# A cross-attention and soft-MoE kernel on one core: new order of loads, layer norm, query products and ctx turns in its opening

## The chip, the cores and the metric

The kernel runs on one core of one Trainium2 chip. The metric is the device time of one execution in microseconds (us); lower is better. The median of three runs of the kernel before is 443.7 us (443.57 to 444.12).

## What is computed

All arrays are float32: `x` is 8 x 56 x 128, `ctx_1024` is 8 x 1500 x 128, Wq, Wk and Wv are 128 x 1024 (16 heads of 64), Wo is 1024 x 128.

```
q = heads(_layernorm(x) @ Wq);  k = heads(ctx @ Wk);  v = heads(ctx @ Wv)
attn = softmax(q @ k.T * 64 ** -0.5)                     # 8 batches, 16 heads, 56 x 1500
x = x + (attn @ v) @ Wo
logits = (_layernorm(x) @ phi_w.T + phi_b).reshape(8, 56, 64, 32)
D, C = softmax(logits, axis=3), softmax(logits, axis=2)
X_tilde = clip(einsum('tznp,tzd->npd', D, x), -33000, 65000)    # of the normalised x
X_tilde = tanh(layernorm over d of X_tilde)
Y_tilde = einsum('npd,ndH->npH', X_tilde, expert_w) + expert_b
x = x + einsum('tznp,npH->tzH', C, Y_tilde)
```

## The kernel before

The five engines have an instruction list each (`@block.sync`, `gpsimd`, `tensor`, `scalar`, `vector`), written out by hand, and semaphores alone order them against each other. An engine takes its list strictly in order, so an instruction that waits holds up everything behind it.

**Attention.** The weights are folded first: `wqk` holds, per head, Wq times Wk transposed (128 x 128), and `wvo` the product of Wv and Wo. So a score is (normalised x) @ wqk @ ctx transposed, and the big per-batch operand is ctx itself. For a batch `b` the 16 x 56 = 896 query rows are cut into NT = 7 tiles of 128 rows (`t`, and `g = 7 b + t`), and the 1500 keys into KB = 3 banks of 500, a bank being 4 chunks (CPB) of 125 keys. Each float32 operand is split into a rounded high part and the rest: ScalarE writes the high part (`hi_ctx`, `hi_qk`, `hi_probs`), VectorE the low part (`lo_ctx`, `lo_qk`, `lo_probs`), and TensorE multiplies hi x hi, hi x lo, lo x hi. A tile is: nine score matmuls into the three `scores` banks (`make_scores`), a row maximum per bank on VectorE (`row_max`), one exponential over 1500 columns on ScalarE (`exp_tile`), twelve transposes of the probabilities (`turn_probs`), and a share of the product with ctx (`context_product`). The scores of tile g+1 wait for the exponential of tile g, since they write the same banks.

**The opening**, which the change rewrites, makes what tile 0 needs. SP's queue issues x, three 125-row thirds of the first ctx (`ctx_raw`, one per bank, 250 KB each), Wv and Wo; ScalarE's queue issues Wq and Wk. VectorE makes the layer norm of x in four columns of two batches each (`layernorm(0, x_sb, 0, NQ)`, NQ = 4; the power -0.5 is on GpSimd, `root`), giving `xn`. TensorE, in order: turns Wq (banks S0, S1) and Wk (S2, T0), turns ctx bank 0, turns the four blocks of `xn` into bank ACC (`xnT`), turns ctx bank 1, makes the head products of the first eight heads (`head_pairs(wqT, wkT, 0, T1, S0)`), turns ctx bank 2, and makes the first quarter of the queries (`make_qk(0, 0)`, four heads for the first pair of batches). Each result is copied out of its bank by ScalarE (counted by `setup_act`) or VectorE (`setup_dve`). `setup_pe` counts TensorE's own steps. Quarter `r` of the queries is needed from the tile that first touches its heads: quarter 0 for tile 0, quarter 1 for tiles 1 and 2, quarter 2 for tile 3, quarter 3 for tile 5.

**The rest of the setup** is spread over the first tiles of batch 0 (`half(0, first=True)`), behind the transposes of the tile before: in tile 0 `make_qk(1)`, the other eight heads' `head_pairs`, half of Wv turned, `make_qk(2)`; in tile 1 the other half of Wv, `make_qk(3)`; in tiles 2 and 3 the four `head_products` for `wvo` and two turns of batch 1's ctx; in tile 4 the third turn. GpSimd makes the untransposed split of ctx (`split_ctx`), which also frees `ctx_raw` for the next load, and from `split_qk(1)` on the queries of later batches.

The lines that matter most, on TensorE before tile 0:

```
turn_ctx(0, 0, 1, first=True)
pe.wait_ge(xn_ready, 1)
for q in range(NQ):
    last = tr(bank(ACC)[:, PT * q:PT * q + PT], xn[:, q, :], ident[0:PT, 0:PT])
last.then_inc(setup_pe, 1)
turn_ctx(0, 1, 0, first=True)
pe.wait_ge(setup_act, 3)
head_pairs(wqT, wkT, 0, T1, S0)
```

Lines in the profile: L355 to L360 are SP's first loads, L1043 and L1044 ScalarE's; L612 `turn_weight`, L591 `turn_ctx`, L646 the turn of `xn`, L628 and L632 `head_pairs`, L597 `make_qk`, L667 to L669 `make_scores`, L679 `turn_probs`, L1057 `hi_ctx`, L1063 and L1064 `hi_qk`, L1050 and L1051 ScalarE's copies, L1083 the exponential, L1275 to L1288 the layer norm, L1299 and L1300 VectorE's copies, L1306 `lo_ctx`, L1313 `lo_qk`, L1320 and L1323 `row_max`.

Of the kernel before, what the change touches and what calls it, by code (L numbers as in the profile page):

```python
# [12 lines left out]
def xattn_softmoe_kernel(  # L13
# [63 lines left out]
    with ExitStack() as ctx:  # L77
# [329 lines left out]
        def _(pool):  # L407
# [117 lines left out]
            root(0, 0, NQ)  # L525
# [54 lines left out]
        def _(pe):  # L580
# [61 lines left out]
            turn_weight(wk_sb, 1, T0)  # L642
            turn_ctx(0, 0, 1, first=True)
            pe.wait_ge(xn_ready, 1)
            for q in range(NQ):
                last = tr(bank(ACC)[:, PT * q:PT * q + PT], xn[:, q, :], ident[0:PT, 0:PT])  # L646
            last.then_inc(setup_pe, 1)
# [1 line left out]
            pe.wait_ge(setup_act, 3)
            head_pairs(wqT, wkT, 0, T1, S0)  # L650
            pe.wait_ge(ctxT_lo, 1)
            turn_ctx(0, 2, 1, first=True)
# [962 lines left out]
```

## Time and profile before

| | us |
|---|---|
| median of three runs (lowest, highest) | 443.7 (443.57, 444.12) |
| the profiled execution, its own time | 445.9 |
| its span in the trace | 444.1 |
| TensorE busy in the span | 426.5 |
| VectorE, ScalarE, GpSimd busy | 332.0, 245.2, 159.8 |

The profiled execution took 445.9 us, 2.2 above the median; 1.8 of its time lie outside the span. All positions below are microseconds from the start of the span. A row of a timeline gives start, duration, engine, line, operation, output and input; a row with `xN` stands for N like instructions, its duration from the first's start to the last's end. In brackets stand the idle time before and what ended it. PE is TensorE's matmul, PEld its weight load, DVE VectorE, ACT ScalarE, POOL GpSimd; SPq and ACTq are the queues of those engines, on which a load is issued.

### The profile page before, as it was taken

Reading aid. Unit: us, or ns where it says so; the run is one execution under the profiler, and the core shown is the slowest. Engines: PE = TensorE matmul, PEld = TensorE weight load, DVE = VectorE, ACT = ScalarE, POOL = GpSimd, SP = SyncE. Lnnn points to the kernel's source line nnn. Section 1 sums busy time; section 2 is a strip of 40 time slices with the busy share of each in tenths; the row PEclk is TensorE's granted clock in tenths of the full one; section 3 lists DMA queues with packets and bytes.
Section 4 is the critical chain, followed back from the end, with each engine's and each line's share of the span. In section 5 each row is a group of like instructions: output and inputs, shape, how many; then the busy total and the mean of one; then the engine's idle time right before and its main releaser. Section 6 shows DMA issues by size and latency. Waiting matters only on the chain.

```text
span 444.1 us, 7406 instructions
## 1 busy us (share of the span) xinstructions
PE 426.5 (96%) x2990; PEld 390.2 (88%) x2990; DVE 332.0 (75%) x606; ACT 245.2 (55%) x413; POOL 159.8 (36%) x88
## 2 busy tenths in 40 slices
PE   3899999999999999999999999999999999899997
PEld 2788899999999999889999998899999888798986
DVE  2567775776687678857898789978988999659871
ACT  2266556566565556655665566556656565533641
POOL 2509800416040213130716134517140342456740
PEclk9999999999999999999999999999999999899999
DMA  8111020014111001110010011000000000296000
GB/s 218 63 70 13 13 78 12 13 71 112 13 13 71 19 12 13 70 19 12 11 74 18 13 11 73 19 13 14 1 19 13 11 2 18 56 243 177 1 1 22
DMA packets 15110, 19.05 MB, mean 43 GB/s; under 512 B 3954, under 2 KB 10882, under 8 KB 15076
## 3 DMA queue, kind: packets, MB, share of 16 engines
q1 hardware_dynamic: 14788, 17.53, 15.1%
q10 hardware_dynamic: 288, 1.05, 0.8%
q8 instruction: 24, 0.39, 0.4%
q14 instruction: 10, 0.08, 0.1%
HBM read 18.32 MB, written 0.26 MB: 42 GB/s over the span
## 4 chain that ended last, share of the span: by engine, by line
PE 78%; DVE 10%; ACT 5%; issue 2%; DMA 2%; POOL 2%; POOLq 1%; ACTq 0%
PE turned L679 15%; PE scores L667 8%; PE acc L699 8%; PE acc L701 8%; PE acc L700 8%; PE scores L669 8%; PE scores L668 8%; PE misc L716 3%; DVE small L1320 2%; PE misc L741 2%; DVE pT_l L1330 2%; PE misc L591 2%; ACT prob L1083 2%; DMA wk_sb<-in_L_xattn_Wk_dram 2%; ACT pT_h L1076 1%
## 5 line engine op out<-in xcount | busy, mean ns | idle before, releaser
L1076 ACT CAST pT_h<-turned 125x512 fp32r<-125x512 f32 x168 | 95.0, 590 | 123.8 <-PE turned L679 123.3
L1330 DVE TENSOR_TENSOR pT_l<-turned,pT_h 125x512 fp32r<-125x512 f32 x168 | 112.3, 687 | 65.6 <-ACT pT_h L1076 64.6
L1320 DVE TENSOR_REDUCE small<-scores 128x1 f32<-128x500 f32 x168 | 108.6, 674 | 7.0 <-PE scores L669 6.6
L679 PE MATMUL turned<-ident,prob 128*125 128x128 f32 x672 | 94.5, 276 | 2.9 <-DVE pT_l L1330 2.6
L679 PEld LDWEIGHTS turned<-ident,prob 128*125 128x125 f32 x672 | 87.5, 187 | 10.3 <-DVE pT_l L1330 4.3
L699 PE MATMUL acc<-pT_h,ctx_nh 125*128 125x256 f32 (+1 forms) x288 | 94.9, 330 | 0.0
L1083 ACT ACTIVATE prob<-scores,small 128x1500 f32<-128x1500 f32 x56 | 84.9, 1516 | 13.0 <-DVE small L1323 12.6
L701 PE MATMUL acc<-pT_h,ctx_nl 125*128 125x256 f32 (+1 forms) x288 | 87.1, 303 | 0.0
L700 PE MATMUL acc<-pT_l,ctx_nh 125*128 125x256 f32 (+1 forms) x288 | 87.0, 302 | 0.0
L667 PE MATMUL scores<-ctx_th,qk_h 128*128 128x500 f32 x168 | 67.8, 403 | 1.9 <-DVE qk_l L1313 1.2
L669 PE MATMUL scores<-ctx_th,qk_l 128*128 128x500 f32 x168 | 65.3, 389 | 0.0
L668 PE MATMUL scores<-ctx_tl,qk_h 128*128 128x500 f32 x168 | 65.0, 387 | 0.0
L699 PEld LDWEIGHTS acc<-pT_h,ctx_nh 125*128 125x128 f32 x288 | 55.3, 192 | 0.0
L700 PEld LDWEIGHTS acc<-pT_l,ctx_nh 125*128 125x128 f32 x288 | 55.2, 192 | 0.0
L701 PEld LDWEIGHTS acc<-pT_h,ctx_nl 125*128 125x128 f32 x288 | 55.0, 191 | 0.0
L427 POOL TENSOR_TENSOR ctx_nh<-ctx_raw,zero 125x1536 fp32r<-125x1536 f32 x8 | 22.0, 2749 | 89.3 <-PE acc L701 83.4
L667 PEld LDWEIGHTS scores<-ctx_th,qk_h 128*128 128x128 f32 x168 | 31.6, 188 | 7.6 <-issue 3.0
L669 PEld LDWEIGHTS scores<-ctx_th,qk_l 128*128 128x128 f32 x168 | 31.5, 188 | 6.4
L668 PEld LDWEIGHTS scores<-ctx_tl,qk_h 128*128 128x128 f32 x168 | 31.7, 189 | 4.4
L501 POOL TENSOR_TENSOR logit<-logit,cmax 112x2048 f32<-112x2048 f32 (+1 forms) x5 | 18.5, 3699 | 34.1 <-DVE cmax L1386 32.5
L431 POOL TENSOR_TENSOR ctx_nl<-ctx_raw,ctx_nh 125x1536 fp32r<-125x1536 f32 x8 | 28.0, 3494 | 0.6
L493 POOL TENSOR_TENSOR logit<-logit,cmax 112x2048 f32<-112x2048 f32 (+1 forms) x4 | 16.5, 4130 | 16.8 <-DVE cmax L1410 16.3
(179 smaller groups left out, 544.1 us busy)
## 6 DMA issues: line engine op xcount, KB each, us to landing
ctx_raw<-in_ctx_dram SPq DMA_DIRECT2D x7, 750.0 KB
rbc<-rden_row SPq DMA_DIRECT2D x15, 128.0 KB, 3.0
rbc<-rden_row SPq DMA_DIRECT2D x8, 192.0 KB, 3.0
eb<-in_L_ffn_expert_b_dram SPq DMA_DIRECT2D x4, 256.0 KB, 5.6
ctx_raw<-in_ctx_dram SPq DMA_DIRECT2D x3, 250.0 KB
wq_sb<-in_L_xattn_Wq_dram ACTq DMA_DIRECT2D x1, 512.0 KB, 5.0
wk_sb<-in_L_xattn_Wk_dram ACTq DMA_DIRECT2D x1, 512.0 KB, 8.3
wv_sb<-in_L_xattn_Wv_dram SPq DMA_DIRECT2D x1, 512.0 KB, 9.1
```

What stands on the lines that cost most here:

```text
L431: gp.tensor_tensor(ctx_nl[a][:, :, :], ctx_raw[:, :, :], ctx_nh[a][:, :, :].bitcast(F32), ALU.subtract).then_inc(ctx_nat, 1)
L667: mm(o, hi, ctx_th[a][:, keys], start=True, stop=False)
L668: mm(o, hi, ctx_tl[a][:, keys], start=False, stop=False)
L669: mm(o, lo, ctx_th[a][:, keys], start=False, stop=True).then_inc(scores_pe, 1)
L679: last = tr(turned[0:CK, m, 128 * c:128 * c + 128], prob[u][:, CK * j:CK * j + CK], ident[:, :])
L699: mm(o, ctx_nh[a][:, j, :], hi, start=(j == 0), stop=False)
L700: mm(o, ctx_nh[a][:, j, :], lo, start=False, stop=False)
L701: last = mm(o, ctx_nl[a][:, j, :], hi, start=False, stop=(j == NC - 1))
L1076: nc.scalar.copy(pT_h[0:CK, PLACES[g // NT % 2][t], CPB * k:CPB * k + CPB, :], turned[0:CK, (KB * u + k) % 2, :].rearrange("p (c r) -> p c ...
L1083: nc.scalar.activation(prob[u][:, :].rearrange("p (k w) -> p k w", k=KB), scores[:, :, 0:KW], ACT.Exp, bias=negmax[:, u:u + 1], accum_out= ...
L1320: m = v.tensor_reduce(bankmax[:, u, k:k + 1], scores[:, k, 0:KW], AX.X, ALU.max)
L1330: v.tensor_tensor(pT_l[0:CK, place, dst, :], turned[0:CK, (KB * u + k) % 2, :].rearrange("p (c r) -> p c r", c=CPB), pT_h[0:CK, place, dst ...
```

## The change

Loads: SP now issues x and Wk. ScalarE issues Wq, then each third of the first ctx as two loads, of rows 0 to 111 and 112 to 124, then Wv and Wo. Layer norm: the first column (the first pair of batches) is made and applied by itself, the other three behind it. TensorE before tile 0: Wq, Wk, one block of `xn`, ctx bank 0, head products, ctx bank 1, query quarter 0 (into bank ACC), and then, behind the wait for the split queries, ctx bank 2; the scores of each bank of tile 0 wait for that bank's ctx alone. The other three blocks of `xn` are turned at the end of tile 0. Wv's turns and query quarters 2 and 3 move to tiles 1 and 2, and the turns of batch 1's ctx to tiles 3 and 4 (two of them in tile 4). ScalarE makes the exponential of tile 0 before its copy of the second half of `wqk`.

```diff
             sp.dma_start(x_sb[:, :, :], x_v).then_inc(x_in, 16)
-            for k in range(KB):
-                chunks = slice(CPB * k, CPB * k + CPB)
-                sp.dma_start(ctx_raw[:, chunks, :], ctx_v[0][:, chunks, :]).then_inc(ctx0_in[k], 16)
-            sp.dma_start(wv_sb[:, :], Wv).then_inc(wvo_in, 16)
-            sp.dma_start(wo_sb[:, :, :], Wo.rearrange("(j p) n -> p j n", p=128)).then_inc(wvo_in, 16)
+            sp.dma_start(wk_sb[:, :], Wk).then_inc(wk_in, 16)
...
             act.dma_start(wq_sb[:, :], Wq).then_inc(wq_in, 16)
-            act.dma_start(wk_sb[:, :], Wk).then_inc(wk_in, 16)
+            for k in range(KB):
+                chunks = slice(CPB * k, CPB * k + CPB)
+                for p0, p1 in ROW_PARTS:
+                    act.dma_start(ctx_raw[p0:p1, chunks, :], ctx_v[0][p0:p1, chunks, :]).then_inc(ctx0_in[k], 16)
+            act.dma_start(wv_sb[:, :], Wv).then_inc(wvo_in, 16)
+            act.dma_start(wo_sb[:, :, :], Wo.rearrange("(j p) n -> p j n", p=128)).then_inc(wvo_in, 16)
...
-            root(0, 0, NQ)
+            root(0, 0, 1)
+            root(1, 1, NQ)
             split_ctx(0, 0, first=True)
...
+                    if g == 0:
+                        pe.wait_ge(ctxT_lo, k + 1)
+                        if k == 0:
+                            turn_ctx(0, 2, 1, first=True)
...
                         if t == 0:
-                            make_qk(1, 1)
-                            pe.wait_ge(setup_dve, 1)
+                            make_qk(1, M0)
                             head_pairs(wqT, wkT, 2, T0, T1)
+                            pe.wait_ge(qk_lo, 1)
+                            pe.wait_ge(xn_ready, 2)
+                            turn_xn(1, NQ)
+                        if t == 1:
+                            pe.wait_ge(xnT_dve, 2)
                             pe.wait_ge(wvo_in, 32)
                             turn_weight(wv_sb, 0, ACC)
-                            pe.wait_ge(setup_act, 5)
-                            pe.wait_ge(setup_dve, 4)
-                            pe.wait_ge(qk_lo, 1)
-                            make_qk(2, 0)
-                        if t == 1:
-                            pe.wait_ge(setup_act, 6)
-                            turn_weight(wv_sb, 1, ACC)
                             pe.wait_ge(qk_lo, 2)
-                            make_qk(3, 1)
+                            turn_weight(wv_sb, 1, M0)
+                            make_qk(2, M1)
...
                         if t == 4:
-                            pe.wait_ge(setup_dve, 7)
-                            turn_ctx(1, 2, 1)
+                            pe.wait_ge(setup_dve, 6)
+                            turn_ctx(1, 1, 1)
+                            pe.wait_ge(ctxT_lo, KB + 1)
+                            turn_ctx(1, 2, 0)
...
             hi_ctx(0, 0, 0, 1)
+            copy_out(5, wqk[:, 0:8:2, :], T1, SCALE)
             hi_ctx(0, 0, 1, 0)
-            copy_out(6, wqk[:, 0:8:2, :], T1, SCALE)
+            hi_qk(0, ACC)
             hi_ctx(0, 0, 2, 1)
-            hi_qk(0, 0)
-            hi_qk(1, 1)
-            copy_out(8, wqk[:, 8:16:2, :], T0, SCALE)
+            hi_qk(1, M0)
...
-            layernorm(0, x_sb, 0, NQ)
-            layernorm_apply(0, x_sb, xn, 0, NQ, xn_ready)
+            layernorm(0, x_sb, 0, 1)
+            layernorm(1, x_sb, 1, NQ)
+            layernorm_apply(0, x_sb, xn, 0, 1, xn_ready)
```

How the order of the instructions moves, from Wk's turns to tile 0 on TensorE. Before:

```order
L612 MATMUL turned<-ident,wk_sb 128x128 x4
L591 MATMUL misc<-ident,ctx_raw 128x125 [waits ctx0_in0]
L591 MATMUL misc<-ident,ctx_raw 128x125 x3
L646 MATMUL acc<-ident,xn 128x112 [waits xn_ready]
L646 MATMUL acc<-ident,xn 128x112 x3
L591 MATMUL misc<-ident,ctx_raw 128x125 [waits ctx0_in1]
L591 MATMUL misc<-ident,ctx_raw 128x125 x3
L628 MATMUL turned<-wkT,wqT 128x128 [waits setup_act]
...
L591 MATMUL misc<-ident,ctx_raw 128x125 [waits ctx0_in2,ctxT_lo]
L591 MATMUL misc<-ident,ctx_raw 128x125 x3
L597 MATMUL misc<-xnT,wqk 128x112 [waits ctxT_lo,setup_dve,setup_act]
L597 MATMUL misc<-xnT,wqk 128x112 x3
L667 MATMUL scores<-ctx_th_61,qk_h_63 128x500 [waits qk_lo,ctxT_lo]
```

The same stretch of TensorE with the change:

```order
L613 MATMUL turned<-ident,wk_sb 128x128 x4
L640 MATMUL acc<-ident,xn 128x112 [waits xn_ready]
L592 MATMUL misc<-ident,ctx_raw 128x125 [waits ctx0_in0]
L592 MATMUL misc<-ident,ctx_raw 128x125 x3
L629 MATMUL turned<-wkT,wqT 128x128 [waits setup_dve,setup_act]
...
L592 MATMUL misc<-ident,ctx_raw 128x125 [waits ctx0_in1]
L592 MATMUL misc<-ident,ctx_raw 128x125 x3
L598 MATMUL acc<-xnT,wqk 128x112 [waits xnT_dve,setup_dve,setup_act]
L598 MATMUL acc<-xnT,wqk 128x112 x3
L592 MATMUL misc<-ident,ctx_raw 128x125 [waits ctx0_in2,ctxT_lo,qk_lo]
L592 MATMUL misc<-ident,ctx_raw 128x125 x3
L675 MATMUL scores<-ctx_th_61,qk_h_63 128x500
```

Three turns of `xn` and one of ctx's banks no longer stand ahead of the head products (L628, now L629), and the third ctx turn stands behind the first query product and behind the wait for `qk_lo`.

ScalarE, from its start to the first exponential. Before:

```order
L1043 DMA wq_sb<-in_L_xattn_Wq_dram 128x1024
L1044 DMA wk_sb<-in_L_xattn_Wk_dram 128x1024
L1051 ACT_TABLE_LOAD
L1051 COPY wqT<-scores 128x512 [waits setup_pe] x2
...
L1063 COPY qk_raw<-misc 128x224 [waits qk_pe]
L1064 CAST qk_h_63<-misc 128x224
L1050 ACTIVATE wqk<-turned 128x4x128 [waits setup_pe]
L1083 ACTIVATE prob_51,small<-scores,small 128x1500 [waits negmax_dve]
```

With the change:

```order
L1053 DMA wq_sb<-in_L_xattn_Wq_dram 128x1024
L1057 DMA ctx_raw<-in_ctx_dram 112x512
L1057 DMA ctx_raw<-in_ctx_dram 13x512
...
L1058 DMA wv_sb<-in_L_xattn_Wv_dram 128x1024
L1059 DMA wo_sb<-in_L_xattn_Wo_dram 128x8x128
L1066 ACT_TABLE_LOAD
...
L1078 COPY qk_raw<-misc 128x224 [waits qk_pe]
L1079 CAST qk_h_63<-misc 128x224
L1098 ACTIVATE prob_51,small<-scores,small 128x1500 [waits negmax_dve]
L1065 ACTIVATE wqk<-turned 128x4x128 [waits setup_pe]
```

Nine loads instead of two stand ahead of the table load, and the copy of `wqk` stands behind the exponential.

## Rows read from the trace of the kernel before

**Rows 1.** The page's first part: busy time, share of the span and instructions of each engine.
```profile
PE 426.5 (96%) x2990; PEld 390.2 (88%) x2990; DVE 332.0 (75%) x606; ACT 245.2 (55%) x413; POOL 159.8 (36%) x88
```

**Rows 2.** Busy time by stretch, cut at the tiles' first scores; the last three: PEclk, DMA share, GB/s.
```profile
core 0: us, PE busy (x) PEld busy (x) DVE busy (x) ACT busy (x) POOL busy (x), PEclk, DMA share, GB/s
0.00:5.80 5.80, 0.00 (x0) 0.02 (x1) 0.00 (x0) 1.28 (x1) 1.21 (x10) 1.00 0.63 187
5.80:9.50 3.70, 1.94 (x8) 1.55 (x8) 1.96 (x12) 1.17 (x2) 1.03 (x1) 1.00 1.03 279
...
18.83:25.33 6.50, 5.94 (x45) 5.02 (x46) 3.27 (x6) 2.83 (x6) 2.33 (x1) 1.00 0.16 56
...
30.31:36.58 6.27, 6.14 (x41) 5.39 (x42) 4.77 (x10) 3.64 (x8) 3.57 (x2) 1.00 0.01 0
...
43.14:49.96 6.82, 6.65 (x43) 5.73 (x44) 5.08 (x9) 4.12 (x8) 6.74 (x5) 1.00 0.01 4
...
70.00:380.00 310.00, 309.04 (x2045) 283.63 (x2044) 249.67 (x439) 181.55 (x299) 100.80 (x37) 1.00 0.11 27
```

**Rows 3.** The chain that ended last, from 0 to 40 us: start, duration, what.
```profile
1.16 8.32 DMA wk_sb<-in_L_xattn_Wk_dram
...
9.52 1.12 PE scores L612 x4
...
11.49 0.83 PE misc L591 x4
12.32 0.75 PE acc L646 x4
...
13.90 0.51 PE turned L628
...
16.52 1.13 PE misc L597 x8
...
18.83 0.47 PE scores L667
```

**Rows 4.** The timeline from 0 to 30 us: the loads' issues, the table load and GpSimd's first split.
```profile
1.15 1.14 SPq L358 DMA_DIRECT2D ctx_raw<-in_ctx_dram  x3
...
1.69 1.28 ACT L1051 ACT_TABLE_LOAD   x1 [1.69 <-PEq L1602]
...
3.06 1.54 SPq L360 DMA_DIRECT2D wo_sb<-in_L_xattn_Wo_dram  x1
...
14.86 2.75 POOL L427 TENSOR_TENSOR ctx_nh<-ctx_raw,zero 125x1536 fp32r<-125x1536 f32 x1 [5.92 <-DMA ctx_raw<-in_ctx_dram]
```

**Rows 5.** The same timeline: turns, copies and splits on TensorE, ScalarE and VectorE.
```profile
5.81 1.94 PE L612 MATMUL scores<-ident,wq_sb 128*128 128x128 f32 x8 [5.81 <-DMA wq_sb<-in_L_xattn_Wq_dram]
...
8.97 1.12 DVE L1288 TENSOR_SCALAR xn<-x_sb,lnmv,lnrs 112x128 f32<-112x128 f32 x4 [1.14 <-POOL lnrs L470]
...
15.57 0.65 PE L591 MATMUL misc<-ident,ctx_raw 125*128 125x125 f32 x4
15.68 0.60 ACT L1050 ACTIVATE wqk<-turned 128x512 f32<-128x512 f32 x1 [1.16 <-PE scores L632]
...
16.87 0.68 DVE L1306 TENSOR_TENSOR ctx_tl<-misc,ctx_th 128x500 fp32r<-128x500 f32 x1 [0.46 <-ACT ctx_th L1057]
17.67 0.35 ACT L1063 COPY qk_raw<-misc 128x224 f32<-128x224 f32 x1 [0.83 <-PE misc L597]
...
18.30 0.39 DVE L1313 TENSOR_TENSOR qk_l<-misc,qk_h 128x224 fp32r<-128x224 f32 x1 [0.75 <-ACT qk_h L1064]
...
21.85 0.16 DVE L1323 TENSOR_REDUCE small<-small 128x1 f32<-128x3 f32 x1
...
23.59 1.50 ACT L1083 ACTIVATE prob<-scores,small 128x1500 f32<-128x1500 f32 x1
```

**Rows 6.** The table by stretch again, while batch 1's ctx is loading alone.
```profile
24.00:26.00 2.00, 1.72 (x11) 1.50 (x12) 0.00 (x0) 2.00 (x5) 0.00 (x0) 1.00 0.32 130
```

**Rows 7.** The timeline from 30 us: the end of GpSimd's split of the weights.
```profile
46.06 0.67 POOL L464 TENSOR_TENSOR xa_l<-xnT,xa_h 128x224 fp32r<-128x224 f32 x1
```

More of the change, by code:

```diff
@@ L592, in turn_ctx, with make_qk @@
                 last.then_inc(ctxT_pe, 1)
-            def make_qk(r, m):
+            def make_qk(r, k):
                 for c in range(4):
-                    last = mm(misc[:, m, PT * c:PT * c + PT], wqk[:, 4 * r + c, :],
+                    last = mm(bank(k)[:, PT * c:PT * c + PT], wqk[:, 4 * r + c, :],
                               xnT[:, 0:PT], start=True, stop=True)
@@ L634, in head_pairs, with turn_xn @@
                 second.then_inc(setup_pe, 1)
+            def turn_xn(q0, q1):
+                for q in range(q0, q1):
+                    last = tr(bank(ACC)[:, PT * q:PT * q + PT], xn[:, q, :], ident[0:PT, 0:PT])
+                last.then_inc(xnT_pe, 1)
             pe.wait_ge(ident_ready, 1)
@@ L642, in _ @@
             turn_weight(wk_sb, 1, T0)
+            pe.wait_ge(xn_ready, 1)
+            turn_xn(0, 1)
             turn_ctx(0, 0, 1, first=True)
[L644 to L647, printed above, removed]
+            pe.wait_ge(setup_act, 3)
+            pe.wait_ge(setup_dve, 1)
+            head_pairs(wqT, wkT, 0, T1, S0)
             turn_ctx(0, 1, 0, first=True)
[L649 to L652, printed above, removed]
             pe.wait_ge(setup_act, 4)
-            pe.wait_ge(setup_dve, 3)
-            pe.wait_ge(ctxT_lo, 2)
-            make_qk(0, 0)
+            pe.wait_ge(setup_dve, 2)
+            pe.wait_ge(xnT_dve, 1)
+            make_qk(0, ACC)
             def make_scores(g, a, t):
@@ L1057, in hi_ctx, with hi_qk @@
                 nc.scalar.copy(ctx_th[a][:, KW * k:KW * k + KW], misc[:, m, 0:KW]).then_inc(ctxT_hi, 1)
-            def hi_qk(r, m):
+            def hi_qk(r, k):
                 act.wait_ge(qk_pe, r + 1)
-                both = misc[:, m, 0:4 * PT].rearrange("p (h b t) -> p b h t", h=4, b=2)
+                both = bank(k)[:, 0:4 * PT].rearrange("p (h b t) -> p b h t", h=4, b=2)
                 nc.scalar.copy(qk_raw[:, 4 * r:4 * r + 4, :], both[:, 1])
@@ L1307, in lo_ctx, with lo_qk @@
                                 ALU.subtract).then_inc(ctxT_lo, 1)
-            def lo_qk(r, m):
+            def lo_qk(r, k):
                 dve.wait_ge(qk_hi, r + 1)
-                both = misc[:, m, 0:4 * PT].rearrange("p (h b t) -> p b h t", h=4, b=2)
+                both = bank(k)[:, 0:4 * PT].rearrange("p (h b t) -> p b h t", h=4, b=2)
                 hs = slice(4 * r, 4 * r + 4)
@@ L1494, in half, with copy_xnT @@
                         if t == 0:
[L1495 to L1497 removed]
+                            lo_qk(1, M0)
+                            copy_out(8, wqk[:, 9:16:2, :], T1, SCALE)
+                            copy_xnT(1, NQ)
                         if t == 1:
[L1499 to L1500 removed]
+                            copy_out(10, wvT[:, 4:8, :], M0)
+                            lo_qk(2, M1)
                         if t == 2:
[L1502 to L1503 removed]
+                            lo_qk(3, M0)
+                            copy_out(12, wvo[:, 8:16:2, :], M1)
                         if t == 3:
[L1505 to L1506 removed]
+                            lo_ctx(1, 1, 0, 0)
+                            copy_out(14, wvo[:, 9:16:2, :], M1)
                         if t == 4:
[L1508 removed]
+                            lo_ctx(1, 1, 1, 1)
+                            lo_ctx(1, 1, 2, 0)
+            def copy_xnT(q0, q1):
+                dve.wait_ge(xnT_pe, 2 if q0 else 1)
+                v.tensor_copy(xnT[:, PT * q0:PT * q1], bank(ACC)[:, PT * q0:PT * q1]).then_inc(xnT_dve, 1)
             copy_out(4, wkT[:, 4:8, :], T0)
+            copy_xnT(0, 1)
+            layernorm_apply(1, x_sb, xn, 1, NQ, xn_ready)
+            copy_out(6, wqk[:, 1:8:2, :], S0, SCALE)
             lo_ctx(0, 0, 0, 1)
[L1512 to L1513 removed]
             lo_ctx(0, 0, 1, 0)
[L1515 removed]
+            lo_qk(0, ACC)
             lo_ctx(0, 0, 2, 1)
[L1517 removed]
             for b in range(B):
```

80 lines of the change are left out of this document (36 added, 44 removed).

## The prediction

> **What bounds the kernel.** I read the page's busy times first: TensorE is busy 426.5 of 444.1 us, the next engine 332.0 [rows 1]. The table by stretch says where the rest is: between 70 and 380 us TensorE idles for 1.0 of 310 us, while in the first 9.5 us it has 1.94 us of work, and in the tile from 18.83 to 25.33 it idles for 0.56 [rows 2]. So the body is bound by TensorE, and the change removes no work of TensorE's. It can only start that work earlier, close gaps in the opening, and do less of it at the slow clock. What it wins there is kept to the end as long as nothing else becomes late, since the body has no slack to swallow it.
>
> The chain of waits gives the opening's order: Wk's load from 1.16 to 9.5, then TensorE without a break (Wk's turns from 9.52, ctx, `xn`, ctx, head products from 13.83), then the copy of `wqk`, the first queries at 16.52, their split, and the scores at 18.83 [rows 3]. Wq's turns had begun at 5.81 and, at 0.22 us each, were all issued by 7.5 [rows 5]. TensorE then stood for 2.0 us for Wk.
>
> The granted clock reads 1.00 throughout [rows 2], but four turns take 1.12 us at 9.52 and 0.65 us at 15.57 [rows 3, 5]. By these durations the engine ran at 1.2 GHz first and was at 2.4 GHz by 15.57.
>
> I compare starts of the tiles. Before, the scores begin at 18.83 (tile 0), 25.33, 30.31, 36.58, 43.14 and 49.96 (tile 5) [rows 2]; the text names the gain at each.
>
> **1. Wk earlier.** By 5.8 us the loads have moved 5.8 x 187 = 1.08 MB and by 9.5 another 3.7 x 279 = 1.03 MB, 2.12 MB in all [rows 2]. ScalarE's queue held only Wq and Wk, 1.05 MB, and the second landed at 9.5: the two queues moved equal amounts. Now SP's queue holds x and Wk, 0.75 MB. If the queues share alike again, Wk has landed when 1.51 MB are through, at 5.8 + 0.43 / 0.279 = 7.3 us. If ctx gets the larger share and is all in before Wk, 2.05 MB are, at 9.3 us. I take 8.0, near the first, because it is what the rows show of the sharing, with something added for ctx's smaller pieces. Wk's turns start at 8.05: gain 1.5 (bounds 2.0, as TensorE is free at 7.5, and 0.2).
>
> The split of ctx into 112 and 13 rows: while a 125-row load runs alone, the DMA share is 0.32 and 130 GB/s move [rows 6], against 1.03 and 279 with many loads [rows 2]: a third of the engines. With all of them on it, ctx's 0.75 MB are in by 9.3 (the far end of step 1), against 14.86, when GpSimd got the last third [rows 4]. TensorE needs the thirds at about 9.9, 12.6 and 15.6, so it doesn't wait for them. The Trainium skill ("DMA: Bandwidth & Descriptors", how many engines) has a load run on the largest number up to 16 that divides its rows, 5 for 125, 16 for 112, 13 for 13: 5 of 16 is 0.31, and the rows agree. The same page's rules for kernel authors speak against two transfers to disjoint halves of the partitions ("Don't bother"), as both use the same engines; by that rule the first third comes no sooner than before, and the result is the third rival's.
>
> **2. Less ahead of the head products.** From Wk's first turn to the head products stood 4.31 us of turns: eight of Wk, four of ctx, four of `xn`, four of ctx [rows 3]. Three of `xn` (three quarters of 0.75) and the second ctx group (0.83) move behind: 4.31 - 0.56 - 0.83 = 2.9, with ends 2.7. The head products start at 10.8 against 13.83. They now also wait for VectorE's copy of Wk's second half, about 0.7 us after the turns at 9.75, hidden by the ctx turns (until 10.75). The layer norm is not late: all four columns were ready at 8.97 + 1.12 = 10.1 [rows 5], the first of them 0.8 before that, and TensorE wants the first at 9.75. Gain 3.0.
>
> **3. To the first scores.** Before, 5.0 us from 13.83 to 18.83. The second ctx group goes into the gap in which TensorE waits for the copy of `wqk` (0.60 us, [rows 5]), where the third stood before: nothing. The third comes behind the split queries and ahead of the first scores: 0.45 us at the full clock (0.65 with the last one's tail, [rows 5]), on the path. Scores at 10.8 + 5.0 + 0.45, less some 0.15 that TensorE no longer waits for `lo_ctx`: 16.1. Gain 2.7.
>
> **4. The third bank.** Its ctx must pass ScalarE (0.58) and VectorE (0.68) after 16.25, so its scores run 17.6 to 18.3, and VectorE's maximum is ready at 19.7 against 22.0 [rows 5]. The split costs 1.1 us between first scores and maximum less what VectorE waited: gain 2.3.
>
> **5. The first exponential.** Before, it began at 23.59, 1.6 after its maximum, behind ScalarE's copy of `wqk` [rows 5]. That copy is now behind it, and `hi_qk(1)` ahead: quarter 1 is multiplied from 18.3, in 1.1 us [rows 3], and its two copies take 0.6 (17.67 to 18.30, [rows 5]). So the exponential starts at 20.0, and tile 1 at 21.75 against 25.33: gain 3.6. TensorE has half a Wv turn (0.45) and a query quarter (0.9) less to do in tile 0 and three turns of `xn` more, and idles some 0.9 us.
>
> **6. Giving back.** What was left out comes later. Tile 1 has one more Wv turn: 5.4 against 4.98 us, gain at tile 2 3.15. Tile 2 has 6.2 us of matmuls and a ScalarE copy of 0.6 ahead of its query copies: 6.35 against 6.27. Tiles 3 and 4 as before: gain at tile 5 2.9 to 3.0. Tile 4 has two ctx groups in place of one: 0.45 on TensorE, but 0.6 on ScalarE and 0.7 on VectorE, each ahead of tile 5's maximum. Tile 5 keeps 2.5 to 2.9.
>
> **What isn't on the path.** GpSimd gets its first split 5 us earlier. Quarter 3's split comes 2 us later, and so `split_qk(1)` and `split_weights`, which were done at 46.7 [rows 7]; batch 1 needs them only seven tiles of some 6 us behind 16.1, at 58. ScalarE issues nine loads, not two, ahead of its table load. At 0.38 us each for six ctx loads (three took 1.14), 0.7 for Wv and 1.54 for Wo [rows 4] it is done at 5.7 and has its table (1.28) by 7.0, when the first turned bank waits: nothing or 0.3, with 2 us of slack at the head products.
>
> **Sum.** 2.7 us of gain at tile 6, carried to the end: the profiled execution would go from 445.9 to 443.2, the median from 443.7 to **441.0**. Bounds: Wk at 7.5 adds 0.5. The clock may rise before the head products, which halves 1.7 us of them and what follows at the slow clock: up to 0.9. That gives 4.1 and 439.6. Wk at 9.3 takes 1.3 and the pile-up in tile 4 up to 0.6: 0.8 and 442.9. Range 439.4 to 443.0.
>
> **Rivals.**
> - *Wk is late again* (ctx on ScalarE's queue takes most of the engines' time). For it: ctx's rows are short pieces and all of them stand in the queue beside Wk. Against it: the equal shares so far. Wk at 9.3, gain 1.4: 442.3. Chance 0.12.
> - *More than the sum*: Wk by 7.5, so that TensorE runs without a gap from 5.8 on and reaches 2.4 GHz some microseconds earlier. For it: before, it had 2 us of standing in that stretch. Gain 3.9: 439.8. Chance 0.18.
> - *The split buys nothing*: a piece of 112 rows goes on few engines like one of 125. The first third is turned at 11.3 as before [rows 3], not at 9.9. Against it: x's and Wk's rows, 112 and 128, ran at the full share of 1.03 [rows 2]. Gain 1.3: 442.4. Chance 0.05.
> - *Given back*: tile 4's second ctx group and the later GpSimd chain cost what was won. For it: VectorE and ScalarE set the pace there more than TensorE (6.65 busy of 6.82, [rows 2]). Against: 2.7 us are a lot for 0.7 us of work. 443.3. Chance 0.05.
> - *Slower: ScalarE is held by its loads.* Wo's issue took 1.54 us, not 0.3 [rows 4], perhaps because the queue was full. If eight of the nine took that, ScalarE is free at 13.5, has its table at 14.8, its three copies by 16.6, and the head products start at 16.7. The path behind them is as in steps 3 to 6: 3.2 us slower, 446.9. It decides from the point at which the head products start later than 13.5, so from ScalarE free at 10.4. Against it: in SP's queue the three ctx issues together took 1.14. Chance 0.05.
>
> **Chances.** Forecast 0.55, the rest as above. A measurement of this kernel can tell about 0.2%, 0.9 us, from no change. Faster takes the forecast and the first three rivals: 0.90. Same 0.05, slower 0.05.
>
> **What the new profile should show.** Wk's turns start at 7.6 to 8.5 (at 9.3, the first rival); head products at 10.8; the first scores at 16.1; the exponential at 20.0; tile 1 at 21.7, tile 5 at 47.1; the body as busy as before. ctx's thirds all in before 10, seen on GpSimd's first split. The table load starts at about 5.7; if it starts after 10, the slower rival holds. I am wrong in substance if tile 1 is early and tile 6 isn't.

## The result and the profile after: 1.2% slower

The changed kernel takes 449.94 us (median of 4 runs, 448.61 to 450.21). The kernel before, beside it, takes 443.81 (443.57 to 444.12). The ratio is 1.0116, 95% interval 1.0087 to 1.0145. The forecast was 441.0, in a range of 439.4 to 443.0: the sign was wrong. The profiled execution of the new kernel took 448.61 with a span of 446.8.

The page's first part of the new kernel, beside [rows 1]:

```profile
PE 427.2 (96%) x2990; PEld 390.4 (87%) x2990; DVE 336.7 (75%) x608; ACT 245.2 (55%) x413; POOL 160.2 (36%) x89
```

TensorE has the same work. VectorE has two instructions more and is busy for 4.7 us more: some instruction of VectorE's has become long. The table by stretch, of the new kernel, shows where TensorE lost its time (after the busy times: PEclk, DMA share, GB/s):

```profile
0.00:9.00 9.00, 2.33 (x10) 1.97 (x11) 1.95 (x11) 2.45 (x3) 2.66 (x12) 1.00 0.78 229
9.00:11.00 2.00, 2.00 (x12) 2.00 (x11) 0.39 (x1) 0.59 (x1) 0.60 (x1) 1.00 1.00 310
11.00:14.00 3.00, 3.00 (x21) 2.45 (x20) 3.00 (x4) 0.94 (x2) 2.92 (x2) 1.00 0.54 137
14.00:17.70 3.70, 0.63 (x5) 0.28 (x3) 3.70 (x4) 0.81 (x2) 2.66 (x1) 1.00 0.00 0
17.70:25.00 7.30, 6.19 (x21) 5.19 (x22) 3.46 (x6) 1.17 (x3) 0.00 (x0) 0.53 0.12 36
...
21.14:28.35 7.21, 6.47 (x38) 5.29 (x37) 4.34 (x8) 2.81 (x6) 0.00 (x0) 0.73 0.26 96
28.35:33.46 5.11, 5.11 (x37) 4.76 (x38) 2.88 (x5) 2.70 (x5) 0.00 (x0) 1.00 0.06 21
33.46:40.24 6.78, 6.78 (x49) 5.97 (x47) 5.03 (x11) 4.44 (x9) 0.00 (x0) 1.00 0.01 0
...
46.84:53.66 6.82, 6.82 (x47) 6.10 (x48) 5.08 (x9) 4.11 (x8) 6.82 (x4) 1.00 0.01 4
53.66:60.21 6.55, 5.98 (x39) 5.26 (x40) 5.05 (x10) 4.10 (x8) 6.47 (x5) 1.00 0.00 0
...
70.00:380.00 310.00, 309.06 (x2046) 283.69 (x2045) 248.38 (x440) 183.22 (x302) 98.41 (x36) 1.00 0.11 28
```

From 14.0 to 17.7 TensorE works for 0.63 us, while VectorE is busy without a break. In the 7.3 us after that the granted clock is 0.53. The first scores (tile 0) start at 21.14, where the kernel before had 18.83 [rows 2], and tile 1 starts at 28.35 against 25.33. The body from 70 to 380 us is as busy as before. By tile 55, the last one (374.63 against 370.39), the kernel is 4.24 us behind.

The chain that ended last names the hole (start, duration, what):

```profile
1.15 7.41 DMA wk_sb<-in_L_xattn_Wk_dram
...
8.60 1.12 PE scores L613 x4
...
11.59 0.51 PE turned L629
...
13.60 1.02 PE misc L592 x4
14.63 3.07 issue
17.69 1.60 PE acc L598 x8
...
21.49 0.42 PE scores L675
```

Wk's turns at 8.60 and the head products at 11.52 to 11.59 are early, against 9.52 and 13.83 to 13.90 [rows 3]. At 14.63 the product for the first queries (`make_qk`, L598) stands for 3.07 us. "issue" gives no releaser. The timeline does:

```profile
7.73 0.34 DVE L1303 TENSOR_SCALAR xn<-x_sb,lnmv,lnrs 112x128 f32<-112x128 f32 x1
...
10.40 2.75 POOL L426 TENSOR_TENSOR ctx_nh<-ctx_raw,zero 125x1536 fp32r<-125x1536 f32 x1 [1.62 <-DMA ctx_raw<-in_ctx_dram]
...
10.61 0.69 DVE L1316 COPY wkT<-turned 128x512 f32<-128x512 f32 x1 [2.54 <-PE turned L613]
11.22 0.26 DVE L1530 COPY xnT<-acc 128x112 f32<-128x112 f32 x1
11.40 5.59 DVE L1303 TENSOR_SCALAR xn<-x_sb,lnmv,lnrs 112x128 f32<-112x128 f32 x3
...
13.23 3.43 POOL L430 TENSOR_TENSOR ctx_nl<-ctx_raw,ctx_nh 125x1536 fp32r<-125x1536 f32 x1
...
16.91 0.68 DVE L1315 TENSOR_SCALAR wqk<-scores 128x512 f32<-128x512 f32 x1
```

The query product needs VectorE's half of the `wqk` copy (L1315). That copy stands behind the three `xn` instructions of the layer norm (L1303), and these take 5.59 us, where four took 1.12 before [rows 5]. The summary of this tile has their durations in ns, as lowest, median and highest:

```profile
L1303 DVE TENSOR_SCALAR xn<-x_sb,lnmv,lnrs x3: 333/1832/3583, 11.4 to 16.7; 112x128 f32<-112x128 f32 x3
```

The 1.83 us from 11.4 on end at about 13.2, where GpSimd's first split instruction (L426) ends; the 3.58 end as its second (L430) does, at 16.66. Behind L430 GpSimd is idle, and the last `xn` takes its usual 0.33. VectorE is shown as busy and not as waiting, so no list of waits points to GpSimd.

Each `xn` instruction reads and writes SBUF, as GpSimd's do. The two copies from PSUM, at 10.61 and 11.22, ran at their usual length beside the same GpSimd instruction. That gave my theory.

**Theory.** The change makes two pieces collide that had never met. The new loads bring ctx in by 10.24 instead of 14.69, which starts GpSimd's split at 10.40 instead of 14.86 [rows 4]. The new order on VectorE puts three quarters of the layer norm behind the copy of Wk, at 11.40. VectorE is then held until each GpSimd instruction ends, TensorE stands for 3.1 us, and the clock falls after that.

**Rivals.** The new loads themselves are at fault; the new order on the engines is; or the split of ctx into 112 and 13 rows is.

### The profile page after: what moved, and what is told of

It reads as the page before. It is cut to its first block, busy times and chain, and to the rows that moved or that the text cites. A ratio compares the mean times of both kernels' runs of the same rounds, so it can differ in the third digit from the quotient of the medians.

```text
span 446.8 us, 7415 instructions
## 1 busy us (share of the span) xinstructions
PE 427.2 (96%) x2990; PEld 390.4 (87%) x2990; DVE 336.7 (75%) x608; ACT 245.2 (55%) x413; POOL 160.2 (36%) x89
## 3 DMA queue, kind: packets, MB, share of 16 engines
q1 hardware_dynamic: 13358, 16.24, 14.2%
## 4 chain that ended last, share of the span: by engine, by line
PE 78%; DVE 10%; ACT 5%; issue 3%; POOL 2%; DMA 2%; POOLq 1%; SPq 0%
PE turned L687 15%; PE scores L675 8%; PE scores L677 8%; PE scores L676 8%; PE acc L707 8%; PE acc L709 8%; PE acc L708 8%; PE misc L724 3%; PE misc L592 2%; DVE small L1336 2%; PE misc L749 2%; DVE pT_l L1346 2%; ACT prob L1098 2%; DMA wk_sb<-in_L_xattn_Wk_dram 2%; ACT pT_h L1091 1%
## 5 line engine op out<-in xcount | busy, mean ns | idle before, releaser
L426 POOL TENSOR_TENSOR ctx_nh<-ctx_raw,zero 125x1536 fp32r<-125x1536 f32 x8 | 22.0, 2750 | 79.6 <-PE acc L709 77.9
L430 POOL TENSOR_TENSOR ctx_nl<-ctx_raw,ctx_nh 125x1536 fp32r<-125x1536 f32 x8 | 27.9, 3489 | 0.6
```

The costliest lines, as they stand in the source:

```text
L430: gp.tensor_tensor(ctx_nl[a][:, :, :], ctx_raw[:, :, :], ctx_nh[a][:, :, :].bitcast(F32), ALU.subtract).then_inc(ctx_nat, 1)
```

## The experiments

Each edit is against the changed kernel, where nothing else is said. "Tile n" is the start of the scores of tile n in the profiled execution. The kernel before was measured beside each of three sets: 443.94 (443.15 to 446.89), 445.46 (442.89 to 446.77) and 443.98 (443.00 to 446.66). Its times fall in two groups (see "The size of the loss"), so its median depends on how many fall in each, and a ratio with its interval isn't the quotient of two medians.

**The layer norm earlier.** The three instructions are moved out of GpSimd's way, nothing else.

```
             layernorm_apply(0, x_sb, xn, 0, 1, xn_ready)
+            layernorm_apply(1, x_sb, xn, 1, NQ, xn_ready)
...
             copy_xnT(0, 1)
-            layernorm_apply(1, x_sb, xn, 1, NQ, xn_ready)
```

> The changed kernel with VectorE applying the layer norm to the last three columns right behind the first, ahead of its copy of Wk's second half, instead of behind the copy of the first column's turn. Theory A (GpSimd's ctx split, from 10.4 to 16.7 us, blocks these three VectorE instructions, which took 1.83, 3.58 and 0.33 us instead of 0.34 each): the three now run at 8.8 to 9.7, 0.34 us each, before the split starts; head products still start at 11.5, the first queries at about 14.4 instead of 17.7, the first scores at 17.2 to 17.6 instead of 21.1, no fall of the clock to 0.5 at 18 us, and the time is 441.5 (440.5 to 442.5). Theory B (the new order of TensorE's work is what costs, the long xn instructions are hidden): no better than 448. Theory C (the arriving loads slow VectorE's reads and writes of SBUF, up to about 13 us): the three are still stretched, as the loads arrive until 13.2 us, the time is above 444.

Measured: 443.07 us (442.11 to 444.90), ratio to before 0.9974 [0.9953, 0.9995]. The timeline:

```profile
8.79 0.86 DVE L1303 TENSOR_SCALAR xn<-x_sb,lnmv,lnrs 112x128 f32<-112x128 f32 x3 [0.75 <-POOL lnrs L470]
10.57 2.74 POOL L426 TENSOR_TENSOR ctx_nh<-ctx_raw,zero 125x1536 fp32r<-125x1536 f32 x1 [1.81 <-DMA ctx_raw<-in_ctx_dram]
...
13.39 3.44 POOL L430 TENSOR_TENSOR ctx_nl<-ctx_raw,ctx_nh 125x1536 fp32r<-125x1536 f32 x1
13.60 0.69 DVE L1316 TENSOR_SCALAR wqk<-scores 128x512 f32<-128x512 f32 x1 [2.08 <-PE scores L633]
```

The same three instructions take 0.86 us, and the first query product starts at 14.40 instead of 17.69. The collision costs 6.9 us by the medians, 5.6 by tile 55 (+4.24 against -1.39). The collision is gone as expected, but the time is 0.6 above my range: the gain over the kernel before is smaller than I thought. The `wqk` copy, also a TENSOR_SCALAR but reading PSUM, takes its usual 0.69 wholly beside L430.

**GpSimd waits instead.** The order on VectorE stays; the split waits until `xn` is written.

```
                 if first:
                     for k in range(KB):
                         pool.wait_ge(ctx0_in[k], 16 * len(ROW_PARTS))
+                    pool.wait_ge(xn_ready, 2)
```

> The changed kernel, but GpSimd's first split of ctx waits until the last three columns of xn are there; VectorE's order is untouched, they still come at 11.4 us. Theory A: they take 0.34 us each, until 12.3, the split runs from 12.4 to 18.6 and nobody waits for it; time 441.5 (440.5 to 442.5), equal to xn_early. Theory B: no better than 448. Theory C: the three are stretched all the same, since the loads still arrive; time above 444.

```profile
11.06 0.85 DVE L1304 TENSOR_SCALAR xn<-x_sb,lnmv,lnrs 112x128 f32<-112x128 f32 x3
12.08 2.75 POOL L427 TENSOR_TENSOR ctx_nh<-ctx_raw,zero 125x1536 fp32r<-125x1536 f32 x1 [3.50 <-DVE xn L1304]
```

442.37 us (441.81 to 444.31), ratio 0.9961 [0.9943, 0.9979]. At the same place in VectorE's order the work takes 0.85 us once GpSimd is quiet. It runs from 11.06 to 11.9, while Wv and Wo are still arriving (until 13.0), so arriving loads don't slow it. So neither the order nor the early loads are slow by themselves, only the two at once.

**Either half of the change alone.** First the kernel before with the new loads (SP: `x`, Wk; ScalarE: Wq, ctx as 112 and 13 rows, Wv, Wo; the waits on ctx counted for two loads):

```
-            act.dma_start(wk_sb[:, :], Wk).then_inc(wk_in, 16)
+            for k in range(KB):
+                chunks = slice(CPB * k, CPB * k + CPB)
+                for p0, p1 in ROW_PARTS:
+                    act.dma_start(ctx_raw[p0:p1, chunks, :], ctx_v[0][p0:p1, chunks, :]).then_inc(ctx0_in[k], 16)
...
```

> The kernel before with the new loads alone (Wk behind x, ctx in pieces of 112 and 13 rows behind Wq, then Wv and Wo); all order on the engines as before. Theory A: all of xn is made at 9.0 to 10.1, before the split can start at 10.4, so nothing is blocked; Wk lands 0.9 us earlier, and that is the gain: 442.9 (442.2 to 443.7), the scores of tile 0 at 17.9. Theory C: other VectorE instructions up to 13 us are stretched. If the new loads are harmful by themselves, it is slower than 443.8.

442.70 us (442.19 to 445.08), ratio 0.9977 [0.9955, 0.9998]; run again in the third set, where I expected 441.8 to 442.6, it took 443.60 (442.31 to 445.22), 0.9983 [0.9962, 1.0004].

Second, the changed kernel with the old loads:

```
-        ROW_PARTS = ((0, 112), (112, CK))
+        ROW_PARTS = ((0, CK),)
...
-            sp.dma_start(wk_sb[:, :], Wk).then_inc(wk_in, 16)
+            for k in range(KB):
+                chunks = slice(CPB * k, CPB * k + CPB)
+                sp.dma_start(ctx_raw[:, chunks, :], ctx_v[0][:, chunks, :]).then_inc(ctx0_in[k], 16)
...
```

> The changed kernel with the loads of the kernel before (Wk behind Wq on ScalarE's queue, ctx in pieces of 125 rows behind x on SP's); all order on the engines as in the change. Theory A: ctx's last third lands at 14.7, the split starts behind it, the three xn instructions at about 12.4 find GpSimd idle and take 0.34 us each; the first scores at about 17.8, time 442.3 (441.3 to 443.5). Theory B: no better than 447. It is the load order that makes the collision, and the VectorE order that exposes it; either alone is not slower than before.

443.81 us (442.97 to 446.13), ratio 1.0001 [0.9978, 1.0024]. The `xn` three are done before GpSimd starts, so they miss each other:

```profile
12.26 0.85 DVE L1302 TENSOR_SCALAR xn<-x_sb,lnmv,lnrs 112x128 f32<-112x128 f32 x3
14.67 2.75 POOL L430 TENSOR_TENSOR ctx_nh<-ctx_raw,zero 125x1536 fp32r<-125x1536 f32 x1 [5.85 <-DMA ctx_raw<-in_ctx_dram]
```

The first scores came at 17.97, about as expected, but the time is 0.3 above my range: the new order wins 0.86 us there and has 0.42 left at tile 55. Neither half is slower, and the two together are 1.2% slower.

**What the clock adds.** 32 turns of the identity into a free bank keep TensorE at work in the hole. The hole itself stays.

```
             turn_ctx(0, 1, 0, first=True)
+            for n in range(32):
+                tr(scores[:, 1, 0:128], ident[:, :], ident[:, :])
```

> The changed kernel with 32 turns of the identity on TensorE (into a free bank, read by nobody) behind the turn of ctx's second third, where it stands for 3.1 us while VectorE is blocked: the stall stays, only the idle time is filled, 32 x 0.11 = 3.5 us. If the fall of the clock to 0.5 from 18.2 to 25.0 us is a second cost beside the stall: the granted clock stays at 1.00, the scores start at 20.9 to 21.4 as in the change, but tile 1 starts at about 26.8 instead of 28.4 and the later tiles 1.5 to 2.5 us sooner than in the change: 447 (445.8 to 448). If the clock costs nothing, the time is the change's 449.9 or more.

446.43 us (446.14 to 447.78), ratio 1.0040 [1.0023, 1.0057]. By stretch:

```profile
14.00:17.70 3.70, 3.59 (x33) 3.35 (x31) 3.70 (x3) 0.70 (x2) 2.87 (x1) 1.00 0.00 0
17.70:25.00 7.30, 5.95 (x45) 4.90 (x45) 4.61 (x10) 2.14 (x6) 0.00 (x0) 1.00 0.16 49
```

VectorE is held as before (5.92 us for the three), but the granted clock stays at 1.00 where it was 0.53. Tile 55 is at +2.27 against +4.24. Of the 5.63 us between the changed kernel and the one with the layer norm earlier, 3.66 are the stall itself and 1.97 are the slow clock behind it. These are differences between three single profiled executions, in which Wk landed within 0.14 us of each other (8.46 to 8.60).

**Is it the kind of instruction?** The same arithmetic in the same place, but with a running sum written out for the three (`accum_out`):

```
+                    acc_out = lnbuf[:, q, 0:1] if n == 1 else None
...
-                                        ALU.subtract, ALU.mult)
+                                        ALU.subtract, ALU.mult, accum_out=acc_out)
```

> The changed kernel, the three blocked VectorE instructions in the form that also writes a sum of its row (into a spent buffer), same operands, same place, GpSimd's split running beside them. If only a form that takes both of VectorE's ports to SBUF is locked out by GpSimd: each takes 0.25 to 0.45 us at 11.4 to 12.5, nobody is blocked, time 442.4 (441.5 to 443.5). If any VectorE instruction from SBUF to SBUF is locked out while GpSimd works on SBUF: 1.8, 3.6 and 0.3 us again and about 449.9.

```profile
10.30 2.75 POOL L426 TENSOR_TENSOR ctx_nh<-ctx_raw,zero 125x1536 fp32r<-125x1536 f32 x1 [1.70 <-DMA ctx_raw<-in_ctx_dram]
...
10.90 0.40 DVE L1304 TENSOR_SCALAR_CACHE_REDUCE xn<-x_sb,lnmv,lnrs 112x128 f32<-112x128 f32 x1
...
11.22 0.40 DVE L1304 TENSOR_SCALAR_CACHE_REDUCE xn<-x_sb,lnmv,lnrs 112x128 f32<-112x128 f32 x1
```

442.81 us (442.07 to 444.23), ratio 0.9959 [0.9939, 0.9979]. All three run in the middle of L426, in 0.40 us each. The collision depends on the form of the instruction, not on SBUF traffic as such.

**And two inputs from SBUF?** The three as two `tensor_tensor` over 384 columns, mean and factor read as a broadcast operand:

```
-            layernorm_apply(1, x_sb, xn, 1, NQ, xn_ready)
+            v.tensor_tensor(xn[:, 1:NQ, :], x_sb[:, 1:NQ, :], lnmv[:, 1:NQ, 0:1].broadcast_to([PT, NQ - 1, D]),
+                            ALU.subtract).then_inc(xn_sub, 1)
...
+            v.tensor_tensor(xn[:, 1:NQ, :], xn[:, 1:NQ, :], lnrs[:, 1:NQ].unsqueeze(2).broadcast_to([PT, NQ - 1, D]),
+                            ALU.mult).then_inc(xn_ready, 1)
```

> The changed kernel, the three blocked instructions replaced by two of VectorE with two SBUF inputs each (x minus the mean, then times the root, 112 x 384), same place, GpSimd's split beside them. The summing form of one input was not blocked. If an instruction that reads two tensors from SBUF is locked out too: the first ends with GpSimd's first instruction at about 13.2, the second with its second at about 16.7, and the time is 449 to 450. If only the form that reads and writes one tensor at double rate is locked out: each takes 0.5 to 0.6 us and the time is 442.7.

```profile
10.33 2.75 POOL L427 TENSOR_TENSOR ctx_nh<-ctx_raw,zero 125x1536 fp32r<-125x1536 f32 x1 [1.46 <-DMA ctx_raw<-in_ctx_dram]
...
11.32 2.17 DVE L1536 TENSOR_TENSOR xn<-x_sb,lnmv 112x384 f32<-112x384 f32 x1
13.16 3.61 POOL L431 TENSOR_TENSOR ctx_nl<-ctx_raw,ctx_nh 125x1536 fp32r<-125x1536 f32 x1
13.53 3.66 DVE L1539 TENSOR_TENSOR xn<-xn,lnrs 112x384 f32<-112x384 f32 x1
```

449.85 us (449.25 to 450.49), ratio 1.0119 [1.0078, 1.0161], as slow as the change. This form is held too, by one GpSimd instruction each. Here the granted clock fell to 0.5 at 15.2, while TensorE still stood, and was back at 25.4; in the changed kernel it was at 0.5 from 18.2 to 25.0.

**ctx in one piece.** `ROW_PARTS = ((0, CK),)` in the changed kernel.

> The changed kernel with each third of ctx as one load of 125 rows, still on ScalarE's queue behind Wq. The last third lands at 13 to 14.5 instead of 10.3, as 5 of 16 engines carry it, so GpSimd's split starts there and the three xn instructions at 11.4 are not blocked: they take 0.34 us each. The first third comes at about 9.5 to 10, in time or 0.3 late. Time 442.8 (441.8 to 444). If the collision does not hang on ctx's arrival, about 449.9.

443.87 us (443.01 to 445.66), ratio 0.9986 [0.9967, 1.0005]. The thirds of ctx land at 10.17, 12.44 and 14.49, in place of 8.78, 9.39 and 10.24: the split into 112 and 13 rows works as the prediction had it. GpSimd now starts at 14.65, after the `xn` three (11.86 to 12.71), and the collision is gone. An edit that slows the loads makes this kernel 1.3% faster.

**Undoing what was given back.** On the kernel with the layer norm earlier: in tile 1 the second queries' copy goes ahead of Wv's, and batch 1's third ctx split goes back from tile 4 to tile 5 on ScalarE and VectorE, as before the change.

```
+                            hi_qk(2, M1)
                             copy_out(9, wvT[:, 0:4, :], ACC)
-                            hi_qk(2, M1)
...
+                        if t == 5:
                             hi_ctx(1, 1, 2, 0)
```

> xn_early with two repairs of what it gives back against loads_only: in tile 1 ScalarE splits query quarter 2 ahead of its copy of half of Wv (tile 2 took 6.78 us against 6.27), and batch 1's last ctx third is split in tile 5 instead of tile 4 (tile 5 took 6.55 against 5.97). If those two are the causes: tile 2 6.3, tile 5 6.0, tile 6 at 53.5 (2.4 us ahead of the kernel before instead of 1.3), time 441.8 (441.0 to 442.6). If the causes are TensorE's own extra work there: tiles 2 and 5 as in xn_early and 443.0.

442.90 us (441.81 to 443.91), ratio 0.9949 [0.9932, 0.9965]; run again, 442.75 (441.29 to 443.98), 0.9956 [0.9935, 0.9977]. By stretch, tile 2 and tile 5 of the second run:

```profile
27.36:34.14 6.78, 6.78 (x49) 5.97 (x47) 5.03 (x11) 4.44 (x9) 0.00 (x0) 1.00 0.01 0
47.56:53.52 5.96, 5.90 (x39) 5.25 (x40) 4.47 (x9) 3.62 (x7) 5.88 (x5) 1.00 0.00 0
```

I had expected 441.8. The second edit works: tile 5 goes from 6.55 to 5.96. The first does nothing, as tile 2 stays at 6.78 with TensorE busy throughout. My cause for tile 2, a late copy on ScalarE, was wrong: it is TensorE's own work that was moved there.

**A Wv turn in the idle time before tile 1.** On that version, the first Wv turn and its copy go to the end of tile 0, where TensorE waits 0.75 us for the first exponential:

```
                             turn_xn(1, NQ)
+                            pe.wait_ge(wvo_in, 32)
+                            turn_weight(wv_sb, 0, M1)
                         if t == 1:
-                            pe.wait_ge(xnT_dve, 2)
-                            pe.wait_ge(wvo_in, 32)
-                            turn_weight(wv_sb, 0, ACC)
...
-                            make_qk(2, M1)
+                            pe.wait_ge(xnT_dve, 2)
+                            make_qk(2, ACC)
...
```

> swap_later with the first half of Wv turned at the end of tile 0 (into bank M1, copied by ScalarE there), in the 0.75 us in which TensorE waits for the first exponential, instead of in tile 1; query quarter 2 goes into bank ACC. Tile 1 takes 0.45 us less (4.7 instead of 5.1) and tile 2 stays bound by TensorE's own work at 6.8: tile 6 starts 2.9 us ahead of the kernel before, against 2.5 in swap_later. Time 0.4 us below swap_later's and 0.7 below loads_only's in the same comparison: 441.4 (440.8 to 442.2). If tile 1 is bound by the exponential and not by TensorE's work: no change against swap_later.

443.49 us (440.95 to 444.63), ratio 0.9977 [0.9955, 0.9998]: no gain over the version without it. Tile 1 took 4.98 and not the 4.7 I wanted. Tile 8 took 7.86 us against 6.87 with the layer norm earlier alone (7.01 and 7.34 in the two executions without this edit). The traces show what it waits for, here and with the layer norm earlier alone:

```profile
71.18 0.69 DVE L1373 TENSOR_TENSOR oT<-acc,rbc 128x384 f32<-128x384 f32 x1 [2.58 <-DMA rbc<-rden_row]
```
```profile
70.34 0.66 DVE L1372 TENSOR_TENSOR oT<-acc,rbc 128x384 f32<-128x384 f32 x1 [0.75 <-DMA rbc<-rden_row]
```

VectorE stands for a small transfer (`rden_row`, then `rbc`: the reciprocals of the softmax sums), and its maxima for the exponential stand behind that. The first half of the transfer is issued on SP's queue right behind batch 2's ctx, at 57.07, and lands 9.7 us later. That ctx load waits for GpSimd's split of batch 1's ctx, which the new order has late: it is issued at 56.3 to 58.1 in all versions with the new order and without the collision, against 53.1 before and 50.9 with the new loads alone. VectorE's wait is 0.4 to 1.1 us in five of these versions, and tile 8 stays at 6.85 to 6.87; with waits of 1.75, 2.06 and 2.58 it takes 7.01, 7.34 and 7.86. No run tries a cure.

**Best version.** The layer norm earlier with the third split in tile 5 beats both kernels, at 442.8 to 442.9, by 0.4 to 0.5% against before. The ones where GpSimd waits (442.37) and with the running sum (442.81) are as good within the intervals.

## Why the prediction was wrong

**The sign: "What isn't on the path. GpSimd gets its first split 5 us earlier."** The section with that sentence costed GpSimd's new times by what they make late and not by what they meet, and put them at nothing. The runs show 5.6 us there: 3.7 of stall and 2.0 of slow clock. Both facts were at hand: the split was released by the last third of ctx [rows 4], which I put at 9.3, and the order of the changed kernel has three `xn` instructions behind the copy of Wk, which I put at about 10.5.

**Step 2, "The layer norm is not late".** It looked at the first column alone, which was indeed ready (7.73 to 8.07). It took the time of the other three from the kernel before (8.97 + 1.12), though the change moves them behind the copy of Wk. Their delay had no term in the sum, neither as order nor as collision. Their place in the order costs little by itself: there the three take 0.85 us when GpSimd is quiet.

The Trainium skill ("SBUF — State Buffer", Who interferes with whom) states this collision: VectorE and GpSimd share one pair of SBUF ports under an exclusive lock, and whoever has it keeps it for a whole instruction; `tensor_scalar` in its two-port mode takes it, the form that writes its accumulator doesn't, and `tensor_tensor` with two SBUF inputs meets GpSimd's reads. The traces agree on all three: 1.83 and 3.58 us, 0.40, and 2.17 and 3.66. It was the rule that speaks against this change, and I weighed another. That a port lock is the mechanism is the page's word; the runs show which forms are held, and until when.

**Steps 1 and 2, right with sizes off.** Wk landed at 8.56 for 8.0 (8.1 to 9.0 over the other kernels with Wk on SP's queue), so its turns began at 8.60. The head products came at 11.52 for 10.8: 0.55 from Wk, and 0.32 in which TensorE stood for VectorE's copy of Wk's second half, which I had called hidden, less 0.15 elsewhere. The copy ended at 11.3, and the ctx turns no longer covered it.

**Steps 3 to 5.** Without the collision, with ctx loaded as changed, the first scores come at 16.2 to 17.0 (forecast 16.1) and tile 1 at 21.9 to 22.75 (21.75). The differences follow Wk's landing, and the clock: from Wk's landing to the first scores it is 8.05 to 8.12 us where TensorE's durations became short by 12.4, and 8.43 to 8.54 where they did so at 13.3 or later. In the profiled execution of the change they were 21.14 and 28.35.

**Step 6, giving back.** Tile 1 took 5.11 (forecast 5.4). Tile 2 took 6.78 (6.35): TensorE is busy throughout, so step 6's "6.2 us of matmuls" is the term that was too small, by 0.6. Tile 5 took 6.55, against 5.97 before, as tile 4's two ctx groups make tile 5's maximum late: 0.58, the upper end I gave. Of 2.7 us forecast, 1.4 are left at tile 55 with the layer norm earlier, 1.7 when GpSimd waits, 2.2 with the running sum. Most of that is the loads' own: the kernel before with the new loads alone has 2.2 in the profiled execution without a fall of the clock. Against it, the kernel with the layer norm earlier wins 0.44 us more by tile 1, though its Wk landed 0.42 later, and gives back 0.14 in tile 1, 0.5 in tile 2 and 0.58 in tile 5.

Measured times say less still. By the runs whose mean granted clock is 1.00, the five versions with the new loads and order and without the collision, and the new loads alone, have medians of 442.3 to 442.9, 0.6 to 1.3 us below the kernel before beside them (443.5 to 443.6). So even without the collision the sum was more than twice too large, and the new order isn't shown to add anything to the new loads.

**The rivals.** ScalarE was not held by its loads. The table load stood at 4.96, earlier than I had put it:

```profile
4.47 0.46 ACTq L1059 DMA_DIRECT2D wo_sb<-in_L_xattn_Wo_dram  x1
4.96 1.28 ACT L1066 ACT_TABLE_LOAD   x1 [4.96 <-issue]
```

The split of ctx did bring it early (the first third at 8.78, in one piece at 10.17), so "the split buys nothing" is out. Wk was not late again (8.56; the rival had 9.3). I had a slower rival with the wrong engine: it looked for one engine that stands in its own queue, not for two that stand in each other's way.

**The size of the loss.** Tile 55 is 4.24 us late and the medians differ by 6.1. Three things lie between.

First, the profiled execution of the change (448.61) is the fastest of its four, 1.3 below their median. The other three had a lower mean granted clock, 0.989 against 0.992. Where they lost it is not on record; the kernel with two inputs from SBUF, also at 0.989, lost it all in the opening.

Second, the clock can also fall in the tail. By stretch, the kernel before, then the changed one:

```profile
382.00:389.00 7.00, 5.64 (x35) 5.58 (x35) 4.79 (x6) 3.80 (x6) 0.69 (x2) 0.76 0.48 101
```
```profile
382.00:389.00 7.00, 5.20 (x37) 4.77 (x37) 3.02 (x6) 4.23 (x7) 4.45 (x1) 1.00 0.00 0
```

From tile 55 to the end of the span it is 73.7 to 73.8 us in the five profiled executions with this fall, before among them, and 72.2 in the nine without, the change among them. So the fall costs 1.5 us, and that is why the two spans differ by only 2.7.

Third, the kernel before lies in two groups. Over the 35 executions of the first set they are 443.15 to 444.34 (mean granted clock 1.00) and 445.42 to 446.89 (0.996), and the 4 runs beside the change were all of the first. The groups' spans have medians of 441.8 and 444.05; of these 2.25 us the tail's fall explains 1.5, and the rest stays open. Less a tail of 72.2, the first group has its tile 55 at about 369.6 (estimate), 0.8 earlier than in the profiled execution of before. So the opening of the change costs 4.2 us against that execution and about 5.0 against the first group, and every position "at tile 55" above flatters its kernel by some 0.8.

So 1.0116 holds for those runs. That the change is slower stands on either reading: its fastest run is 1.7 us above the slowest of the second group. Kernels within 0.3% of each other can't be told apart by their medians here, and single profiled executions, 2.6 us apart for one program (below), are no sure guide either.

## What to carry to other kernels

When a transfer arrives earlier, ask what it releases on GpSimd and which VectorE instructions then run beside it: those that work from SBUF to SBUF, in the plain form or with two inputs, can stand for a whole GpSimd instruction, here 0.9 us of work for 5.6. Writing out the running sum avoids it. Look for this in the durations of busy instructions, since no wait shows it, and cure it by order: the short VectorE piece first, or GpSimd's start behind it. Count a stall of TensorE's with the slow clock behind it: here 3.7 us of stall brought 2.0 more. Ask too what the later times of an engine off the path release: a later GpSimd split held back a ctx load and with it a small transfer, and cost up to 1.0 us 50 us further on.

## What the hardware showed that was not expected

- A VectorE `tensor_scalar` of 112x128 from SBUF to SBUF took 0.33 us alone and up to 3.58 us beside a GpSimd instruction; the same instruction with an accumulator took 0.40 us beside it, and copies and `tensor_scalar` from PSUM their usual 0.26 to 0.69. ScalarE's copies weren't touched (0.60 for `wqk`, as in [rows 5]).
- GpSimd, which ran on while VectorE was held, was hardly slower: L426 took 2.75 us in all kernels, L430 3.43 in the changed one and 3.48 with nothing beside it; only beside the form with two inputs from SBUF did it take 3.61.
- The granted clock can also fall without such a stall. The same kernel (before with the new loads) had it at 1.00 in one profiled execution, with tile 1 at 23.19; in the other it fell from 17.76 on, with tile 1 at 25.83. In the second, by stretch:

```profile
17.70:25.00 7.30, 6.96 (x42) 5.86 (x43) 3.27 (x6) 2.00 (x4) 0.00 (x0) 0.77 0.29 107
```

TensorE stood for 1.20 us ahead of the first scores in both. What differed ahead of the fall is when its durations became short: a head product took 0.27 us from 12.5 on in the first, and in the second still 0.42 at 14.0 and 0.32 at 14.2. Whether that decided it stays open. It is 2.6 us between two executions of one program, more than most edits here are worth.
